# Cross-attention and an eight-expert FFN on one core: x turned earlier, FFN weights prepared over eleven groups, and the expert mask moved from TensorE to VectorE

## The chip, the core and the metric

The kernel runs on one core of a Trainium2 chip. The metric is the device time of one execution in microseconds (us). A core has TensorE (PE in the profile; PEld is its weight loads), VectorE (DVE), ScalarE (ACT), GpSimd (POOL) and the DMA queue of SyncE (SP). They run side by side and meet at semaphores.

## The reference

Input is `x` of 128 batches of 128 tokens by 256, and a context of the same shape. All arithmetic is float32.

```python
x = x + xattn(layernorm(x), ctx, ctx, ...)      # 16 heads of 16
x = x + ffn(layernorm(x), ...)                  # 8 experts, hidden 64

# the FFN, xt being the tokens:
logits = xt @ Wg.T
top1 = argmax(logits)                           # one expert per token
xhat = layernorm without scale
for each expert e:
    h = gelu((xhat * s_e + b_e) @ w1 + bb1)
    y += (top1 == e) * (h @ w2 + bb2)
```

## The kernel before

The batches are worked in 32 groups of four (`GB = 4`, so 512 tokens). A first phase does the attention of all groups and stores `x2` in device memory; a second does the FFN of all groups. Every engine has its own program in a fixed, hand-written order; semaphores join them.

**Attention.** A group has eight steps (`u` from 0 to 7), one per batch and half of the heads. In a step TensorE makes the scores of the unit three ahead (`scores`, L999), the transposed scores (`scoresT`, L1027), and one or two of the ten `item`s of a later group (items 0 and 1 turn the normalised x, 2 and 3 turn the context, 4 to 7 are the query and key projections, 8 and 9 the values), and in even steps the value products `values` (L1041) of the batch before. ScalarE does the exponentials (L593), keeps the turned x (`item(n + 2, 0)`, L557) and normalises the x of the group two ahead (`normalise`, L576, four pieces). VectorE takes the row maxima (`maxima`, L744, L747, L749) that gate the next scores, and the low parts of x and context (`lower`, L770). A float32 operand is kept as two parts, high and low, and multiplied in three products.

VectorE also prepares the FFN weights during attention (`ffn_weights`): per quarter (a *chunk*) a scaling for the first two, a high part and a low part, in steps 4, 5 and 6 of groups 1 to 4; six small ones on the gate weights and `b2` in steps 0 to 6 of group 5.

**FFN.** All eight experts' hidden units (4 pieces `m` of 128 rows, so two experts per piece) are computed for every token, and those of the experts not chosen have to come out as zero. For that, `mask` (L1223) adds to the sum in PSUM one more product per piece, of `far_sel` with `offhotT` (one-hot minus one), which puts −2^30 on every expert that is not chosen; gelu makes it zero. In a group TensorE does `hidden` (24 products of 512 columns, L1216), four of `mask`, `output` (48 products of 256 columns, L1235, and four for the bias, L1238), the turning of the next x (L1182), `gate` (L1191), `turn_logits` (L1197) and `turn_onehot` (L1203). ScalarE does the gelus (L647), keeps the one-hot rows twice (`keep_onehot`, L636, as `offhotT`; `keep_onehot_by_e`, L639, as `onehotT`), keeps the turned x (L632) and copies x2 into the output buffer (L653). VectorE splits each hidden piece into its high part (L853) and low part (L855), normalises the x of the next group (L311, four pieces), takes its statistics (L298, L304), picks the expert (`route`, five small instructions) and adds the output (`add`, L847). GpSimd works out the scale of the normalisation (`ffn_norm`, L504 to L516) and one low part of x (L520). The DMA queue loads x2 (L275) and stores the output (L281).

Of the kernel before, what the change touches and what calls it, by code (L numbers as in the profile page):

```python
# [29 lines left out]
def xattn_moe(nc, x, ctx_in, wq, bq, wk, bk, wv, bv, wo, bo, wg, ln_s, ln_b, w1, b1, w2, b2, out):  # L30
# [13 lines left out]
    assert T == P and D == 256 and GROUPS % 2 == 0 and GROUPS > 4 and GROUPS * GB == BATCH  # L44
# [19 lines left out]
    with ExitStack() as stack:  # L64
# [84 lines left out]
        onehot = sb("onehot", [P, GB, 3, EP], BF16)  # L149
        onehotT = [sb(f"onehotT{n}", [3 * EP, GT], BF16) for n in range(2)]  # L150
        offhotT = [sb(f"offhotT{n}", [3 * EP, GT], BF16) for n in range(2)]
# [92 lines left out]
        f_ld = [sem(f"ffn_x2_loaded{n}") for n in range(2)]  # L244
# [12 lines left out]
        o_ps = [st_ps[:, 0:D], st_ps[:, 512:512 + D]]  # L257
# [11 lines left out]
        def ffn_load(sp, n):  # L269
            src = x2_v[n]  # L270

            wait(sp, f_xn, at(GB, n - 2, GB))
            wait(sp, f_cp, at(1, n - 2, 1))
            sp.wait_ge(st_x2[n % 2], (n // 2 + 1) * 16)
            sp.dma_start(xin[n % 2][:], src).then_inc(f_ld[n % 2], 16)  # L275

        def ffn_sync(sp):
            def store(n):
                dst = out_v[n]
                sp.wait_ge(f_out, at(GB, n, GB))  # L280
                sp.dma_start(dst, xb[n % 2][:]).then_inc(f_st[n % 2], 16)  # L281

            def group(n):
                if n + 3 <= LAST:
                    ffn_load(sp, n + 3)
                store(n)

            ffn_load(sp, 2)
            for n in range(GROUPS):
                group(n)  # L290
            for n in range(2):
                sp.wait_ge(f_st[n], 8 * GROUPS)

        def ffn_stats_of(dve, n):
            v = nc.vector
            dve.wait_ge(f_ld[n % 2], (n // 2 + 1) * 16)
            for b in range(GB):
                v.bn_stats(stats[:, b, :], xin[n % 2][:, b, :]).then_inc(f_bn, 1)  # L298

            for b in range(GB):  # L300
# [5 lines left out]
        def ffn_normalise(dve, n):  # L306
# [3 lines left out]
            for b in range(GB):  # L310
                v.tensor_scalar(xn[:, b, :], xin[n % 2][:, b, :], mv[:, b, 0:1], rstd[:, b:b + 1],  # L311
# [6 lines left out]
        def _(sp):  # L318
# [74 lines left out]
            def group(g):  # L393
# [3 lines left out]
                if 1 <= g <= 4:  # L397
                    load_chunk(g - 1)
# [30 lines left out]
        def _(pool):  # L429
# [70 lines left out]
            def ffn_norm(n):  # L500
# [4 lines left out]
                pool.wait_ge(f_v1, one)  # L505
                g.tensor_tensor(rstd[:], ve[:], neg_half[:], ALU.pow).then_inc(f_r1, 1)
# [9 lines left out]
                g.tensor_tensor(rstd[:], rstd[:], rstd2[:], ALU.mult).then_inc(f_r12, 1)  # L516

# [7 lines left out]
            lo_of_xT(0)  # L525

            def ffn_group(n):
                more = n < LAST
                if n + 2 <= LAST:
                    ffn_norm(n + 2)  # L530
                if more:
                    lo_of_xT(n + 1)
# [6 lines left out]
        def _(act):  # L539
# [31 lines left out]
            def normalise(n):  # L571
                act.wait_ge(s_shift, at(1, n, 1))

                wait(act, s_pp, at(ITEMS, n - 1, 2))
                for b in range(GB):
# [58 lines left out]
            def keep_onehot(n):  # L634
                act.wait_ge(f_ot, at(1, n, 1))
                a.activation(offhotT[n % 2][:], onehotT_ps(n), ACT.Copy, bias=-1.0).then_inc(f_ote, 1)  # L636
# [12 lines left out]
            def copy(n):  # L649

                act.wait_ge(f_ld[n % 2], (n // 2 + 1) * 16)
                wait(act, f_st[n % 2], (n // 2) * 16)
                a.copy(xb[n % 2][:], xin[n % 2][:]).then_inc(f_cp, 1)  # L653

            def group(n):
                more, more2 = n < LAST, n + 2 <= LAST
                for u in range(UNITS):
                    nxt = later(n, u, 2)
                    done = turned_at(n, u)
                    if done and u % 2 == 0:  # L660
                        keep_attn(*done)
                    if u % 2 == 0 and turned_at(n, u + 1):
                        keep_pvT(*turned_at(n, u + 1))
                    if more2 and u == 4:
                        item(n + 2, 0)
# [7 lines left out]
                    if more2 and u == 3:  # L673
                        normalise(n + 2)
# [18 lines left out]
            keep_attn(LAST, GB - 1)  # L693
            def ffn_group(n):
                if n > 0:
                    keep_onehot(n)
                gelu(n, 0)
                gelu(n, 1)
                if n > 0:
                    keep_onehot_by_e(n)  # L700
                if n < LAST:
                    for c in range(C):
                        keep_xT(n + 1, c)
                for m in range(2, MC):
                    gelu(n, m)
                if n < LAST:
                    if n == 0:
                        act.wait_ge(st_x2[1], 8 * GROUPS)
                    copy(n + 1)

            for n in range(GROUPS):
# [4 lines left out]
        def _(dve):  # L716
# [67 lines left out]

            def ffn_weights(n, u):
                last = slice(2 * EP, 3 * EP)
                if n in (1, 2) and u == 4:
                    full = w_chunk[:].rearrange("p (e h) -> p e h", h=HID)
                    dve.wait_ge(s_wf, 16 * n)
                    v.tensor_tensor(full, full, ecols[:, n - 1, E:2 * E].unsqueeze(2).broadcast_to([P, E, HID]),  # L790
                                    ALU.mult).then_inc(s_ffw, 1)
                elif n in (1, 2, 3, 4) and u == 5:
                    dve.wait_ge(s_wf, 16 * n)
                    wait(dve, s_ffw, FFW_FREE[n - 1] + (n < 3))
                    v.tensor_copy(ffn_chunk(n - 1, 0).bitcast(F32R), w_chunk[:]).then_inc(s_ffw, 1)
                elif n in (1, 2, 3, 4) and u == 6:
                    wait(dve, s_ffw, FFW_FREE[n - 1] + (n < 3) + 1)
                    v.tensor_tensor(ffn_chunk(n - 1, 1).bitcast(F32R), w_chunk[:], ffn_chunk(n - 1, 0),
                                    ALU.subtract).then_inc(s_ffw, 1)
                elif n == 5 and u == 0:  # L800
                    v.memset(wg_pad[:].rearrange("p c e -> p (c e)"), 0.0).then_inc(s_ffw, 1)
                elif n == 5 and u == 1:
                    dve.wait_ge(s_ffw, FFW - 6)
                    v.tensor_copy(wg_pad[:, :, 0:E], ecols[:, :, 0:E]).then_inc(s_ffw, 1)
                elif n == 5 and u == 2:
                    dve.wait_ge(s_b2, 16 * 3)
                    v.tensor_copy(b2p[:], b2f[:]).then_inc(s_ffw, 1)
                elif n == 5 and u == 3:
                    dve.wait_ge(s_ffw, FFW - 4)
                    v.tensor_tensor(b2r[:], b2f[:], b2p[:], ALU.subtract).then_inc(s_ffw, 1)  # L810
                elif n == 5 and u in (4, 5):
                    part = slice((u - 3) * EP, (u - 2) * EP)
                    dve.wait_ge(s_ffw, FFW - 3)
                    v.tensor_copy(b2p[part, :], b2r[part, :]).then_inc(s_ffw, 1)
                elif n == 5 and u == 6:
# [26 lines left out]
            def add(n, b):  # L842
# [4 lines left out]
                v.tensor_tensor(xr, xr, o_ps[b % 2], ALU.add).then_inc(f_out, 1)  # L847

            def split_hidden(n, m):

                dve.wait_ge(f_he, at(MC, n, m + 1))
                hi, lo = hT_hi[n % 2][:, m, :], hT_lo[n % 2][:, m, :]
                v.tensor_copy(hi.bitcast(F32R), hidden32[m]).then_inc(f_hh, 1)  # L853
                dve.wait_ge(f_hh, at(MC, n, m + 1))
                v.tensor_tensor(lo.bitcast(F32R), hidden32[m], hi, ALU.subtract).then_inc(f_hl, 1)  # L855
# [105 lines left out]
            residual(LAST, GB - 1)  # L961
            def ffn_group(n):
                more = n < LAST
                if 0 < n < LAST:
                    ffn_normalise(dve, n + 1)
                if 0 < n <= LAST - 2:
                    ffn_stats_of(dve, n + 2)
                for m in range(MC):
                    split_hidden(n, m)
                if n == 0:  # L970
                    ffn_stats_of(dve, 2)
                add(n, 0)
                if more:
                    split_xT(n + 1)
                add(n, 1)
                if more:
# [365 lines left out]
```

## Time and profile before

| | |
|---|---|
| median of 3 runs | 1468.85 us (1468.51 to 1470.84) |
| the profiled execution | 1470.98 us, its span 1468.8 us |
| mean granted TensorE clock | 0.992 |
| PE busy | 1409.6 us, 96% |
| PEld busy | 1206.0 us, 82% |
| DVE busy | 1172.8 us, 80% |
| ACT busy | 866.1 us, 59% |
| POOL busy | 465.4 us, 32% |

The span runs from the first to the last instruction; the execution's own time holds 2.2 us more. A busy share is the mean over two phases with different limits, so each phase is looked at by itself. Starts of instructions count from the span's start. An instruction's row says what ended the idle time before it, behind an arrow.

### The profile page before, as it was taken

How to read it: one execution, taken by the hardware profiler on the slowest of the kernel's cores; microseconds unless marked ns; L12 is line 12 of the kernel's file. 1: busy time of each engine (PE TensorE's matmuls, PEld its weight loads, DVE VectorE, ACT ScalarE, POOL GpSimd, SP SyncE). 2: the span in 40 equal slices, each digit the busy share in tenths (PEclk: the TensorE clock that was granted, in tenths of full speed). 3: DMA queues.
4: the chain of work that ended last, by engine and by line, in shares of the span. 5: the costliest groups of instructions: out<-in, count | busy, mean ns of one | idle time of the engine just before them, and what ended most of it. 6: DMA issues, size and time to landing. Idle time of an engine off the chain costs nothing.

```text
span 1468.8 us, 39587 instructions
## 1 busy us (share of the span) xinstructions
PE 1409.6 (96%) x15438; PEld 1206.0 (82%) x15438; DVE 1172.8 (80%) x2880; ACT 866.1 (59%) x1451; POOL 465.4 (32%) x602
## 2 busy tenths in 40 slices
PE   6799999999999999999999999989999999999998
PEld 5688878888888888888888888867888888888887
DVE  4688888888888888888888888777777777777775
ACT  5466667777777777777777777753343333334342
POOL 4222322223223332323232323223333343433340
PEclk8899999999999999999999999999999999999999
DMA  7566755566556656665666566512222222221211
GB/s 187 119 161 174 178 154 147 158 167 177 154 162 172 179 143 174 171 178 145 169 174 168 146 167 172 156 32 87 72 73 73 73 73 73 72 73 64 81 59 43
DMA packets 150480, 190.89 MB, mean 130 GB/s; under 512 B 17631, under 2 KB 101146, under 8 KB 150298
## 3 DMA queue, kind: packets, MB, share of 16 engines
q1 hardware_dynamic: 150298, 188.38, 47.2%
q8 instruction: 125, 2.05, 0.6%
q14 instruction: 57, 0.47, 0.1%
HBM read 53.01 MB, written 33.55 MB: 59 GB/s over the span
## 4 chain that ended last, share of the span: by engine, by line
PE 73%; DVE 14%; issue 6%; ACT 6%; DMA 1%; POOL 0%; SPq 0%; ACTq 0%; DVEq 0%
PE st_ps L1235 13%; PE s_ps L1216 12%; PE pp_ps L1093 9%; DVE negmax L744 6%; PE s_ps L999 6%; PE pp_ps L1066 6%; PE st_ps L1027 6%; PE pv_ps L1041 5%; PE pp_ps L1101 4%; PE pv_ps L1049 3%; DVE cT_lo L770 3%; ACT xn L576 2%; PE s_ps L1223 2%; PE pp_ps L1182 2%; DVE negmax_wide L747 2%
## 5 line engine op out<-in xcount | busy, mean ns | idle before, releaser
L593 ACT ACTIVATE pT<-st_ps 128x1024 f32<-128x1024 f32 x256 | 263.1, 1028 | 130.3 <-PE st_ps L1027 130.3
L744 DVE TENSOR_REDUCE negmax<-s_ps 128x8 f32<-128x1024 f32 x256 | 311.3, 1216 | 29.1 <-PE s_ps L999 28.9
L1235 PE MATMUL st_ps<-w_hi,q_packed 128*128 128x256 f32 x1024 | 215.8, 296 | 0.2
L472 POOL TENSOR_TENSOR xb<-xin,bo_all 128x256 f32<-128x256 f32 x128 | 91.2, 734 | 273.8 <-DMA x_scratch<-xb 163.1
L1235 PEld LDWEIGHTS st_ps<-w_hi,q_packed 128*128 128x128 f32 x1024 | 167.8, 189 | 10.3 <-issue 6.0
L999 PE MATMUL s_ps<-k_packed,q_packed 96*128 96x128 bf16 x2048 | 157.9, 220 | 18.5 <-issue 8.3
L1216 PE MATMUL s_ps<-k_packed,w_hi 128*128 128x512 f32 x512 | 171.5, 423 | 0.6 <-ACT pT L647 0.6
L460 POOL TENSOR_TENSOR q_parts<-q,q_parts 128x1024 bf16<-128x1024 f32 x32 | 68.5, 2141 | 298.5 <-ACT q_parts L587 298.5
L1027 PE MATMUL st_ps<-q_packed,k_packed 98*128 98x128 bf16 x2048 | 158.4, 220 | 2.5 <-DMA q_packed<-negmaxT 2.4
L999 PEld LDWEIGHTS s_ps<-k_packed,q_packed 96*128 96x128 bf16 x2048 | 127.5, 98 | 39.4 <-DVE negmax L744 20.0
L636 ACT ACTIVATE offhotT<-pv_ps 96x512 bf16<-96x512 bf16 x31 | 18.4, 592 | 222.8 <-PE pv_ps L1203 222.8
L1027 PEld LDWEIGHTS st_ps<-q_packed,k_packed 98*128 98x128 bf16 x2048 | 120.5, 98 | 29.8 <-issue 26.1
L1235 PE MATMUL st_ps<-w_lo,q_packed 128*128 128x256 f32 x512 | 142.4, 278 | 0.0
L1041 PE MATMUL pv_ps<-pT,v 128*32 128x128 f32 x4096 | 138.6, 276 | 0.0
L647 ACT ACTIVATE pT<-s_ps,c 128x512 f32<-128x512 f32 x128 | 84.6, 686 | 67.0 <-PE s_ps L1223 66.1
L551 ACT COPY uvT<-pv_ps 128x512 f32<-128x512 f32 x128 | 75.2, 587 | 76.3 <-PE pv_ps L1041 76.3
L1041 PEld LDWEIGHTS pv_ps<-pT,v 128*32 128x32 f32 x4096 | 104.1, 109 | 13.4 <-issue 0.3
L778 DVE TENSOR_TENSOR xb<-xb,pp_ps 128x256 f32<-128x256 f32 x128 | 53.5, 418 | 65.1 <-PE pp_ps L1066 65.1
L853 DVE CAST q_packed<-pT 128x512 fp32r<-128x512 f32 x128 | 54.5, 425 | 59.1 <-ACT pT L647 59.1
L1216 PEld LDWEIGHTS s_ps<-k_packed,w_hi 128*128 128x128 f32 x512 | 89.9, 191 | 14.1 <-ACT pT L647 1.1
L1235 PEld LDWEIGHTS st_ps<-w_lo,q_packed 128*128 128x128 f32 x512 | 96.6, 189 | 0.8
L847 DVE TENSOR_TENSOR xb<-xb,st_ps 128x256 f32<-128x256 f32 x128 | 53.7, 420 | 50.9 <-PE st_ps L1238 50.7
(181 smaller groups left out, 3489.7 us busy)
## 6 DMA issues: line engine op xcount, KB each, us to landing
q_packed<-q_parts SPq DMA_DIRECT2D x192, 256.0 KB, 3.9
k_packed<-k_parts SPq DMA_DIRECT2D x192, 256.0 KB, 4.6
xin<-in_x_dram SPq DMA_DIRECT2D x32, 512.0 KB, 3.9
cin<-in_ctx_dram SPq DMA_DIRECT2D x32, 512.0 KB, 4.0
x_scratch<-xb SPq DMA_DIRECT2D x32, 512.0 KB, 4.6
xin<-x_scratch SPq DMA_DIRECT2D x32, 512.0 KB, 3.8
out_dram<-xb SPq DMA_DIRECT2D x32, 512.0 KB, 2.9
q_packed<-negmaxT SPq DMA_DIRECT2D x128, 8.0 KB
```

The lines of the kernel that those rows point to most:

```text
L472: last = g.tensor_tensor(xb[n % 2][:, b, :], xin[n % 2][:, b, :], bo_all[:], ALU.add)
L551: a.copy(uvT[:], pv_ps[:]).then_inc(s_uv, 1)
L593: a.activation(pT[u % 2][:], st_ps[:], ACT.Exp, scale=DH ** -0.5).then_inc(s_exp, 1)
L647: a.activation(hidden32[m], h_ps[m % 2], ACT.Gelu, bias=c1[:, m:m + 1]).then_inc(f_he, 1)
L744: v.tensor_reduce(own, s_ps[:].rearrange("p (h s) -> p h s", s=P), AX_X, ALU.max, negate=True).then_inc(s_red, 1)
L999: mm = t.matmul(s_ps[:, j * P:(j + 1) * P], packed[0][n % 2][0:KP, slot(m, j), tok], packed[1][n % 2][0:KP, slot(m, j), tok], start=True, ...
L1027: mm = t.matmul(st_ps[:, j * P:(j + 1) * P], packed[1][n % 2][0:KP + 2, slot(m, j), tok], packed[0][n % 2][0:KP + 2, slot(m, j), tok], sta ...
L1041: mm = t.matmul(pv_ps[strip:strip + HP, block:block + P], v1[n % 2][:, b, h, :], pT[m][:, j * P:(j + 1) * P], start=True, stop=True)
L1066: mm = t.matmul(y_ps, aT[b % 2][i][:, c, :].bitcast(F32R), woT[j][:, c, :].bitcast(F32R), start=(c == 0 and i == j), stop=(c == C - 1 and ...
L1093: mm = t.matmul(ps[:], w[i][:, c, k % 2 * P:(k % 2 + 1) * P].bitcast(F32R), src[j][:, c, :].bitcast(F32R), start=(c == 0 and i == j), stop ...
L1216: t.matmul(h_ps[m % 2], w[:, c, e, :].bitcast(F32R), x[n % 2][:, c, :].bitcast(F32R), start=(k == 0 and c == 0), stop=False)
L1235: t.matmul(o, h[n % 2][:, m, tok].bitcast(F32R), w[:, m, :].bitcast(F32R), start=(m == 0 and k == 0), stop=False)
```

## The change

In attention, at step 4 TensorE turns the first half of the next x (item 0) before the value products, and ScalarE keeps it before it keeps the value products' result; ScalarE's four normalisations move apart, two at the end of step 2 and two in step 3. The FFN weights are prepared over groups 1 to 11, at steps 3 and 6, by the same instructions, and their four loads go out in groups 1, 3, 5 and 7.

In the FFN the four `mask` products go, except in group 0. In their place the one-hot rows, 0 and 1 in bfloat16, are copied by DMA to the 64 rows of each expert: a group has eight copies (`load_mask`), each of one row of `onehotT` to 64 rows of `mask_rows`, which lie in buffers that attention no longer uses. VectorE multiplies each gelu result by them (`mask_hidden`). ScalarE makes the high part of the hidden pieces (`hidden_hi`) and normalises x (`ffn_normalise_by_shift`), and keeps the one-hot rows once. Routing runs one group earlier and the x2 loads have five buffers. The outputs of all four batches are summed side by side in four banks.

```diff
+            def load_mask(n):
+                sp.wait_ge(f_oh, at(1, n, 1))
+                wait(sp, f_hm, at(MC, n - 3, MC))
+                for m in range(MC):
+                    for e in range(EC):
+                        row = EC * m + e
+                        sp.dma_start(mask_rows[n % 2][e * HID:(e + 1) * HID, m, :],
+                                     onehotT[n % 2][row:row + 1, :].unsqueeze(1).broadcast_to([1, HID, GT])
+                                     ).then_inc(f_ml[m // 2], 16)
             def group(n):
-                if n + 3 <= LAST:
-                    ffn_load(sp, n + 3)
+                if n + XF <= LAST:
+                    ffn_load(sp, n + XF)
+                if n < LAST:
+                    load_mask(n + 1)
                 store(n)
...
@@ ScalarE, attention
+                    if more2 and u == 4:
+                        item(n + 2, 0)
                     if u % 2 == 0 and turned_at(n, u + 1):
                         keep_pvT(*turned_at(n, u + 1))
-                    if more2 and u == 4:
-                        item(n + 2, 0)
...
                     if more2 and u == 3:
-                        normalise(n + 2)
+                        normalise(n + 2, range(GB // 2, GB))
...
+                    if more2 and u == 2:
+                        normalise(n + 2, range(GB // 2))
...
@@ ScalarE, FFN
+            def keep_onehot_by_e(n):
+                act.wait_ge(f_ot, at(1, n, 1))
+                for loaded in f_ml:
+                    wait(act, loaded, ML * (n - 2))
                 a.copy(onehotT[n % 2][:], onehotT_ps(n)).then_inc(f_oh, 1)
+            def hidden_hi(n, m):
+                act.wait_ge(f_hm, at(MC, n - 1, m + 1))
+                a.copy(hT_hi[n % 2][:, m, :].bitcast(F32R), hidden32[m]).then_inc(f_hh, 1)
             def ffn_group(n):
-                if n > 0:
-                    keep_onehot(n)
                 gelu(n, 0)
+                hidden_hi(n, 0)
                 gelu(n, 1)
...
+                hidden_hi(n, 1)
+                gelu(n, 2)
+                gelu(n, 3)
+                hidden_hi(n, 2)
                 if n < LAST:
+                    keep_onehot_by_e(n + 1)
+                hidden_hi(n, 3)
                 if n < LAST:
                     copy(n + 1)
+                if n + 3 <= LAST:
+                    ffn_normalise_by_shift(n + 3)
...
@@ VectorE, FFN
+            def mask_hidden(n, m):
+                dve.wait_ge(f_he, at(MC, n, m + 1))
+                dve.wait_ge(f_ml[m // 2], ML * n)
+                v.tensor_tensor(hidden32[m], hidden32[m], mask_rows[n % 2][:, m, :], ALU.mult).then_inc(f_hm, 1)
...
@@ TensorE, FFN
             def ffn_group(n):
+                hidden(n, 0)
                 if more:
                     gate(n + 1)
+                hidden(n, 1)
                 if more:
                     turn_logits(n + 1)
+                if n + 2 <= LAST:
+                    for c in range(C):
+                        turn(n + 2, c)
+                hidden(n, 2)
+                hidden(n, 3)
+                outputs(n, range(GB), 0)
+                if more:
+                    turn_onehot(n + 1)
+                for m in range(1, MC):
+                    outputs(n, range(GB), m)
```

The order of instructions as built shows three places.

TensorE in attention, step 4 of an inner group, before (`scores` of the unit ahead, then from `values` on):

```order
L999 MATMUL s_ps<-k_packed,q_packed 128x128 x8
L1041 MATMUL pv_ps<-pT,v 32x128 x16
L1027 MATMUL st_ps<-q_packed,k_packed 128x128 x8
L1087 MATMUL pp_ps<-ident,xn 128x128 x4
L1066 MATMUL pp_ps<-woT_hi,aT_hi 128x256 x2
```

and after the change:

```order
L1113 MATMUL s_ps<-k_packed,q_packed 128x128 x8
L1201 MATMUL pp_ps<-ident,xn 128x128 x4
L1155 MATMUL pv_ps<-pT,v 32x128 x16
L1141 MATMUL st_ps<-q_packed,k_packed 128x128 x8
L1180 MATMUL pp_ps<-woT_hi,aT_hi 128x256 x2
```

The four transposes of x stand ahead of the value products and the transposed scores.

ScalarE in one inner group of the FFN, before (pT is the gelu's output, k and q the turned x):

```order
L636 ACTIVATE offhotT<-pv_ps 96x512
L647 ACTIVATE pT<-s_ps,c 128x512 x2
L639 COPY onehotT<-pv_ps 96x512
L632 COPY q<-pp_ps 128x512 x2
L647 ACTIVATE pT<-s_ps,c 128x512 x2
L653 COPY xb<-xin 128x1024
```

and after the change (q_packed holds the high and low parts of the hidden pieces):

```order
L690 ACTIVATE pT<-s_ps,c 128x512
L700 CAST q_packed<-pT 128x512
L690 ACTIVATE pT<-s_ps,c 128x512
L672 COPY q<-pp_ps 128x512 x2
L700 CAST q_packed<-pT 128x512
L690 ACTIVATE pT<-s_ps,c 128x512 x2
L700 CAST q_packed<-pT 128x512
L682 COPY onehotT<-pv_ps 96x512
L700 CAST q_packed<-pT 128x512
L696 COPY xb<-v 128x1024
L706 ACTIVATE xn<-xin,shift,rstd 128x256 x4
```

The copy of the next group's one-hot rows (L682) stands behind the third high part (L700) of this group, which needs this group's third masked piece.

The DMA queue in one inner group of the FFN, before:

```order
L275 DMA xin<-x_scratch 128x4x256
L281 DMA out_dram<-xb 128x4x256
```

and after:

```order
L286 DMA xin<-x_scratch 128x4x256
L300 DMA k_parts<-onehotT 64x1x512 x8
L292 DMA out_dram<-xb 128x4x256
```

Eight copies of one row to 64 rows stand between the load and the store of each group (k_parts and q_parts in turn are the mask rows).

## Rows read from the trace of the kernel before

**Rows 1.** Busy time by stretch: attention twice, then FFN; columns as its head says.

```profile
core 0: us, PE busy (x) PEld busy (x) DVE busy (x) ACT busy (x) POOL busy (x), PEclk, DMA share, GB/s
70.00:220.00 150.00, 140.84 (x1809) 123.26 (x1811) 127.77 (x287) 104.00 (x176) 43.40 (x50) 0.99 0.63 163
220.00:950.00 730.00, 713.12 (x9325) 624.10 (x9314) 622.99 (x1396) 528.14 (x897) 216.42 (x246) 1.00 0.62 164
1100.00:1400.00 300.00, 300.00 (x2201) 247.60 (x2200) 227.77 (x665) 114.37 (x185) 118.02 (x164) 1.00 0.22 71
```

**Rows 2.** Timeline of the FFN: one-hot copy and mask products, group by group.

```profile
1200.21 0.59 ACT L636 ACTIVATE offhotT<-pv_ps 96x512 bf16<-96x512 bf16 x1 [7.17 <-PE pv_ps L1203]
...
1201.46 0.60 PE L1223 MATMUL s_ps<-offhotT,far_sel 96*128 96x512 bf16 x2
...
1201.91 1.04 PE L1182 MATMUL pp_ps<-ident,xn 128*128 128x128 f32 x8
...
1215.05 0.59 ACT L636 ACTIVATE offhotT<-pv_ps 96x512 bf16<-96x512 bf16 x1 [7.17 <-PE pv_ps L1203]
```

**Rows 3.** Groups of the FFN, 1000 to 1440 us: busy us, mean ns of one.

```profile
L855 DVE TENSOR_TENSOR q_packed<-pT,q_packed 128x512 fp32r<-128x512 f32 x116 | 80.4, 693 | 4.0
L853 DVE CAST q_packed<-pT 128x512 fp32r<-128x512 f32 x117 | 49.8, 426 | 52.1 <-ACT pT L647 52.1
L311 DVE TENSOR_SCALAR xn<-xin,mv,rstd 128x256 f32<-128x256 f32 x120 | 41.6, 409 | 0.0
L632 ACT COPY q<-pp_ps 128x512 f32<-128x512 f32 x30 | 16.2, 599 | 0.0
```

**Rows 4.** Waits of attention, 220 to 950 us: total, times, longest.

```profile
DVE xT_lo L770 <- ACT xT_hi L557: 14.8, 25, 0.7
PEld s_ps L999 <- DVE negmax L744: 10.5, 42, 0.8
PE pp_ps L1066 <- DVE cT_lo L770: 10.1, 25, 0.6
```

**Rows 5.** Timeline of one inner attention group, steps 3 and 4.

```profile
654.57 1.02 ACT L593 ACTIVATE pT<-st_ps 128x1024 f32<-128x1024 f32 x1 [1.00 <-PE st_ps L1027]
655.49 2.06 ACT L576 ACTIVATE xn<-xin,shift,rstd 128x256 f32<-128x256 f32 x4
658.72 0.59 ACT L557 CAST xT_hi<-pp_ps 128x512 fp32r<-128x512 f32 x1
659.34 0.69 DVE L770 TENSOR_TENSOR xT_lo<-pp_ps,xT_hi 128x512 fp32r<-128x512 f32 x1 [0.59 <-ACT xT_hi L557]
```

**Rows 6.** DMA issues: count, KB each, median us from issue to landing.

```profile
out_dram<-xb SPq DMA_DIRECT2D x32, 512.0 KB, 2.9
q_packed<-negmaxT SPq DMA_DIRECT2D x128, 8.0 KB
```

**Rows 7.** Short windows around a copy into two rows, into 16 rows, and a store.

```profile
603.82:604.05 0.23, 0.23 (x4) 0.17 (x2) 0.23 (x1) 0.23 (x1) 0.23 (x2) 1.00 0.16 36
614.50:614.90 0.40, 0.40 (x6) 0.35 (x3) 0.40 (x1) 0.40 (x2) 0.00 (x0) 1.00 0.98 179
...
1214.20:1216.20 2.00, 2.00 (x13) 1.49 (x11) 2.00 (x7) 0.59 (x1) 0.00 (x0) 1.00 0.70 241
```

**Rows 8.** Timeline, the first FFN group: gelu, and the first hidden piece's high part.

```profile
992.01 1.27 ACT L647 ACTIVATE pT<-s_ps,c 128x512 f32<-128x512 f32 x2
...
993.66 0.42 DVE L853 CAST q_packed<-pT 128x512 fp32r<-128x512 f32 x1
```

**Rows 9.** Timeline, the end of the span: last addition and last store.

```profile
1464.91 0.42 DVE L847 TENSOR_TENSOR xb<-xb,st_ps 128x256 f32<-128x256 f32 x1 [1.07 <-PE st_ps L1238]
1465.36 0.37 SPq L281 DMA_DIRECT2D out_dram<-xb  x1
```

**Rows 10.** Timeline of attention group 5: a stretched instruction beside a GpSimd one.

```profile
211.41 2.13 POOL L460 TENSOR_TENSOR k_parts<-k,k_parts 128x1024 bf16<-128x1024 f32 x1
211.42 2.15 DVE L749 TENSOR_TENSOR negmax_wide<-negmax,negmax_wide 128x8 bf16<-128x8 f32 x1
```

More of the change, by code:

```diff
@@ L149, in xattn_moe @@
         onehot = sb("onehot", [P, GB, 3, EP], BF16)
+        v_rows = v1[0][:].rearrange("p b h d -> p (b h d)").rearrange("p (k b d) -> p k b d", k=2, b=GB)
+        xf = [xin[0][:], xin[1][:], cin[:], v_rows[:, 0, :, :], v_rows[:, 1, :, :]]
+        XF = len(xf)
+        mask_rows = [part[:, 0:MC // C, :, :].rearrange("p a c t -> p (a c) t") for part in parts]
         onehotT = [sb(f"onehotT{n}", [3 * EP, GT], BF16) for n in range(2)]
-        offhotT = [sb(f"offhotT{n}", [3 * EP, GT], BF16) for n in range(2)]
+        offhotT = sb("offhotT", [3 * EP, GT], BF16)
         def psum(name, shape, dt=F32):
@@ L569, in item, with normalise @@
                 last.then_inc(s_pe, 1)
[L571 to L575, printed above, removed]
+            def normalise(n, batches=range(GB)):
+                if batches[0] == 0:
+                    act.wait_ge(s_shift, at(1, n, 1))
+                    wait(act, s_pp, at(ITEMS, n - 1, 2))
+                for b in batches:
                     a.activation(xn[:, b, :], xin[n % 2][:, b, :], ACT.Identity, bias=shift[:, b:b + 1],
@@ L785, in ffn_weights, with chunk_lo @@
+            def chunk_lo(k):
+                dve.wait_ge(s_ffw, FFW_FREE[k] + (k < C) + 1)
+                v.tensor_tensor(ffn_chunk(k, 1).bitcast(F32R), w_chunk[:], ffn_chunk(k, 0),
+                                ALU.subtract).then_inc(s_ffw, 1)
             def ffn_weights(n, u):
                 last = slice(2 * EP, 3 * EP)
[L787 to L800, printed above, removed]
@@ L1221, in mask, with output @@
+            def mask(m):
                 if m == 0:
[L1222 to L1223 removed]
+                    pe.wait_ge(f_ote, 1)
+                t.matmul(h_ps[m % 2], far_sel[:, EC * m:EC * (m + 1), :], offhotT[:],
                          start=False, stop=True).then_inc(f_h, 1)
[L1226 to L1227 removed]
+            def output(n, b, m):
+                o = o_ps(n, b)
@@ L1228, in output @@
                 tok = slice(b * T, (b + 1) * T)
-                if parts[0] == 0:
-                    wait(pe, f_out, at(GB, n, b - 1))
-                for m in parts:
-                    if b == 0:
-                        pe.wait_ge(f_hl, at(MC, n, m + 1))
-                    for k, (h, w) in enumerate(((hT_hi, w2_hi), (hT_hi, w2_lo), (hT_lo, w2_hi))):
-                        t.matmul(o, h[n % 2][:, m, tok].bitcast(F32R), w[:, m, :].bitcast(F32R),
-                                 start=(m == 0 and k == 0), stop=False)
@@ L1237, in output @@
-                if parts[-1] == MC - 1:
+                if m == 0:
+                    if n == 0:
+                        wait(pe, f_out, b - 1)
+                    else:
+                        pe.wait_ge(f_out, at(GB, n - 1, b + 1 if n > 1 or b > 1 else b + 3))
+                    if n > 0 and b >= 2 and n + 2 <= LAST:
+                        pe.wait_ge(f_tre, at(C, n + 2, b - 1))
+                if b == 0:
+                    pe.wait_ge(f_hl, at(MC, n, m + 1))
+                for k, (h, w) in enumerate(((hT_hi, w2_hi), (hT_hi, w2_lo), (hT_lo, w2_hi))):
+                    t.matmul(o, h[n % 2][:, m, tok].bitcast(F32R), w[:, m, :].bitcast(F32R),
+                             start=(m == 0 and k == 0), stop=False)
```

255 lines of the change are left out of this document (169 added, 86 removed).

## The prediction

> **What bounds the kernel now.** I read the windows by phase first, since the page's shares mix two phases. In [rows 1] the reader sees that in the FFN (1100 to 1400 us) PE is busy 300.00 of 300 us, DVE 227.8, ACT 114.4, POOL 118.0, and the DMA engines 0.22 of their time at 71 GB/s. The timeline [rows 2] gives the period of an FFN group: the one-hot copy L636 starts at 1200.21 and at 1215.05, so 14.84 us. TensorE alone sets it. In attention PE is busy 713.12 of 730 us between 220 and 950 us, and 140.84 of 150 us before that, so 16.9 and 9.2 us of idle time are all there is to win without taking work away. The waits [rows 4] say who makes the first: TensorE waits for the row maxima (10.5 us for its weight loads) and for the low part of the context (10.1 us), both VectorE's.
>
> **Attention, part by part.** VectorE waits 14.8 us in 25 groups, 0.6 each, for the turned x that ScalarE keeps [rows 4]. [rows 5] show one: L557 starts at 658.72, VectorE's L770 behind it at 659.34 after 0.59 idle. What makes it late is the four normalisations from 655.49 on (2.06 us) and the place behind the value products. Half of them move into the 1.00 us that ScalarE idles before its exponential at 654.57, and the transposes move ahead of the products. VectorE gets up to 0.6 us per group, the two waits of TensorE shrink, and I take half of the 16.9 us: 8. The weight preparation is the same VectorE work, spread thinner; of the 9.2 us of idle time before 220 us, 5.7 are above the later rate (150 x 16.9/730 = 3.5), and I take 2. Part of those 5.7 is one collision, where a 0.17 us VectorE instruction takes 2.15 us beside GpSimd's 2.13 us one [rows 10]; other places of such instructions can lose or meet it. Sum −10, bounds 0 (another wait takes over) and −26 (all idle time).
>
> **FFN, what leaves TensorE.** Two mask products start at 1201.46 and the next thing at 1201.91 [rows 2]: 0.225 us each, 0.9 for four. If nothing else bound, a group would take 14.84 − 0.9 = 13.9 us. VectorE loses four high parts (4 x 0.426) and four normalisations (4 x 0.409) and gains four multiplications of the kind of L855 (4 x 0.693) [rows 3]: −0.6 on 11.3 us a group (227.8 of 300). ScalarE gains four casts of 512 columns (about 0.6, as L632) and four normalisations (a quarter of 2.06 each), less one copy: +3.9 on 5.7 us. Both fit 13.9. GpSimd gains two small instructions.
>
> **FFN, what comes in: eight copies.** Each reads one row of `onehotT` (512 values of bfloat16, 1 KB) and writes 64 rows, 64 KB. The trace has no copy out of one row, so I bound it. From below: the store moves 241 GB/s with the DMA engines busy 0.70, so 344 GB/s at full share, 21.5 per engine [rows 7]; 65.5 KB in 0.2 us, which the 0.4 us of an issue [rows 9] hides. From above by copies that meet in few rows. The copy of the row maxima into two rows moves 36 GB/s [rows 7]. The packing copy into 16 rows, alone at 614.50, moves 179 GB/s at a share of 0.98, so 11.4 GB/s per engine, half of the store's 21.5. I read this as two engines that meet at one place in the memory, which then gives 22.8 GB/s together. In the new copies all engines read one row, so they all meet. I take their nearest rows, not the store: 22.8 to 36, and within that 26.6, since the copy from 128 rows also has 16 engines at work but its engines pass on to other rows. That is 65.5/26.6 = 2.46 us a copy, 19.7 us for eight, with 14.6 and 23.0 as bounds.
>
> The Trainium skill speaks to this. "SBUF — State Buffer", section "Door 1: the DMA port swizzle", has the partitions share 16 ports by fours, and measures 27.6 GB/s for a transfer that touches partitions 0 to 3 alone; rows 0 to 3 would be one port and 4 to 7 another. Its figure would make an estimated 2.37 us a copy and 19.0 for eight, and the end 1698 us. Its section "The DMA setup-cost knee" has a formula by bytes alone, 2 us + bytes/436 GB/s, by which the copies would hide, and the end be that of the first rival.
>
> **What waits for them.** `load_mask(n + 1)` goes out when ScalarE has kept the one-hot rows of group n + 1. That copy stands behind `hidden_hi(n, 2)`, which waits for the third masked piece of group n, which waits for the second half of group n's copies. So there is a loop: copies, mask, high part, keep, copies. Behind the waiting `mask_hidden` on VectorE are all later low parts, the split of the next x and the additions; TensorE's `output` waits for those. The fixed part of a DMA is 2.9 us from issue to landing of a store [rows 6] less 524 KB at 344 GB/s, 1.5, so 1.4. Mask 0.69, high part 0.60, keep 0.58, and 0.3 for the handovers (an estimate, a few at 0.05 to 0.1). The loop takes 1.4 + 19.7 + 2.2 = 23.3 us against 14.84. The x2 load and the store, 1.5 us each, go through the same engines in the 3.6 us of the loop without mask data. TensorE will idle some 9 us of each group; its granted clock was 0.94 in the stretch that holds the collision, where one wait was 1.7 us, so it will fall here too, but it is not in the loop.
>
> **The sum**, against the profiled execution. VectorE's first high part starts at 993.66 [rows 8]. Then about 2.0 us of statistics that now stand ahead, four splits of 1.12 (4.5), 0.3 for logits, 0.8 for the last of the outputs of two batches, 0.4 for the turning and 0.6 for keeping: `load_mask(1)` at 1002.3, less the 10 of attention 992.3. There are 31 loads: 30 loops (699), the last load (1.4 + 19.7 = 21.1), and the end: two masks 1.4, high and low part 1.3, the last quarter of the outputs 1.6, an addition 0.4, and 3.4 from the store's issue at 1465.36 to the span's end [rows 9], together 8.1. The span is 992.3 + 699 + 21.1 + 8.1 = 1720.5; +2.2 around it, and −2.1 for the profiled 1470.98 against the median 1468.85: 1720.6 us. With 14.6 us of copies the loop is 18.2 and the end 1562; with 23.0 it is 26.6 and the end 1823.
>
> **Rivals.** *The copies are hidden.* If rows can be read by all engines at a good rate, they go out at 0.4 us each [rows 9] and land within 5 us, and the first half is due some 6.5 us after the one-hot rows are kept (three quarters of the outputs and the first hidden piece lie between). Then TensorE sets the period: 13.9 us, −0.9 x 31 = −28, and −10 from attention: 1431 us. It decides at the point where the loop equals 14.84: eight copies in 11.2 us, 1.4 each, 47 GB/s out of one row. For it speaks that the store's engines run at full speed side by side; against it the halved engines of the packing copy and the 36 GB/s into two rows. Chance 0.20. *Handovers eat the gain.* The copies hide, but the split of a hidden piece now goes VectorE, ScalarE, VectorE, and the last low part comes close. TensorE has the fourth hidden piece 7.3 us into a group (24 products at 0.23 are 5.6, gate and turns 1.7) and wants the last low part 4.5 us later, at 11.8. That part is ready at 10.9: gelu and mask 1.6, the two high parts and the one-hot copy that ScalarE does in turn 1.3 more, low part 0.7. Slack 0.9 us. Two casts late put up to 1 us back in each group: 1431 + 31 = 1462, and the middle 1447. Chance 0.07, of which 0.02 within 0.2% of no change. *The loop binds* as above, chance 0.73.
>
> **How the numbers follow.** The likeliest case gives 1720.6, its own range being 1560 to 1823. To leave no more than 2 in 10 out, the range has to reach to the other cases: 1430 to 1800. What differs by less than 0.2% (3 us) can't be told from no change here. Faster 0.25, same 0.02, slower 0.73.
>
> **What would show it.** Right: one period of about 23 us in the FFN, VectorE's masks waiting for the DMA that writes the mask rows, TensorE busy some 60%, DMA share high for most of a group at a low GB/s (about 27 for the copies alone), issue to landing growing from copy to copy. Wrong: a period of 13.9 to 14.8 us with no wait for these copies. In attention: VectorE's wait for the turned x gone, TensorE's waits at L999 and L1066 (in the old numbering) smaller, and the idle time before 220 us spread. The number falls with the rate out of one row: each 1 GB/s around 26.6 is worth about 23 us.

## The result, and the profile after

The changed kernel takes 1676.06 us (median of 4 runs, 1674.09 to 1676.81) against 1468.97 for the kernel before on the same chip: ratio 1.1405, 95% interval 1.1388 to 1.1423. It is 207 us slower.

The page of its profiled execution (span 1672.2 us): busy time, 40 slices, the chain that ended last.

```profile
PE 1457.9 (87%) x15314; PEld 1252.7 (75%) x15314; DVE 1166.5 (70%) x2760; ACT 992.6 (59%) x1664; POOL 446.3 (27%) x662
...
PE   6999999999999999999999887777777777777776
...
PEclk9999999999999999999999998888888888889888
DMA  6576656656565666757565447777777777777765
GB/s 179 134 186 152 179 148 175 176 156 171 150 179 153 175 169 160 185 149 178 147 179 153 129 73 75 74 75 75 75 75 75 73 66 67 72 75 75 63 49 57
...
PE 44%; DMA 18%; SPq 18%; DVE 13%; issue 4%; ACT 3%; DVEq 0%; ACTq 0%
```

The reader is to see two lines against each other: in the FFN (the right half) the DMA engines are busy seven tenths of the time, and yet move 75 GB/s; in attention they move twice that at six tenths. And 36% of the chain that ended last now runs through transfers (DMA) and through the issues of SP's queue (SPq).

Windows of attention and FFN, which answer to [rows 1] (columns as there):

```profile
70.00:220.00 150.00, 146.90 (x1919) 127.95 (x1916) 131.62 (x295) 110.16 (x187) 45.12 (x53) 1.00 0.65 166
220.00:950.00 730.00, 715.58 (x9307) 624.55 (x9305) 626.71 (x1410) 533.54 (x895) 216.62 (x246) 1.00 0.63 164
...
1100.00:1400.00 300.00, 225.28 (x1445) 189.42 (x1445) 152.30 (x403) 131.24 (x222) 70.63 (x140) 0.87 0.77 71
```

TensorE's idle time fell from 9.2 to 3.1 us in the first and from 16.9 to 14.4 in the second. In the FFN no engine is full. The waits from 1000 to 1600 us say for what they stand still:

```profile
ACT q_packed L700 <- DVE pT L940: 208.1, 56, 6.4
...
PE t_ps L1314 <- DVE logitT L928: 131.5, 28, 5.1
DVE pT L940 <- DMA q_parts<-onehotT: 124.3, 28, 5.7
DVE pT L940 <- DMA k_parts<-onehotT: 121.0, 27, 5.5
```

L940 is `mask_hidden`; it waits 245 us for the copied rows (`q_parts` and `k_parts` are the two buffers of `mask_rows`), ScalarE waits for it in `hidden_hi`, and TensorE for the logits, whose copy stands behind the mask in VectorE's order. One loop, in the chain that ended last (start, length, what):

```profile
1249.68 0.70 DVE pT L940
1250.39 0.02 issue
1250.41 0.04 ACT q_packed L700
1250.45 0.48 issue
1250.94 0.58 ACT onehotT L682
1251.52 0.02 issue
1251.54 0.47 SPq L300
...
1253.33 1.62 SPq L300
1254.95 0.04 issue
1254.99 2.36 SPq L300
1257.35 0.04 issue
1257.39 2.36 SPq L300
1259.75 0.04 issue
1259.80 1.90 SPq L300
1261.69 0.04 issue
1261.73 9.44 DMA k_parts<-onehotT
...
1271.27 0.70 DVE pT L940
```

From mask to mask it is 21.6 us, and the starts of L682 give a mean period of 21.67 (14.84 before, [rows 2]). From the first issue (1251.54) to the last landing (1271.17) it is 19.6 us, all the rest 2.0. The fifth and sixth issue take 2.36 us each, and 65.5 KB in 2.36 us are 27.8 GB/s: in this loop the queue takes a new copy only as fast as an old one leaves. Short windows in the middle of the copies show the rate:

```profile
1256.00:1258.00 2.00, 2.00 (x23) 1.30 (x22) 1.47 (x8) 0.69 (x1) 0.37 (x2) 1.00 0.79 26
1258.00:1260.00 2.00, 0.99 (x5) 0.46 (x3) 0.00 (x0) 0.00 (x0) 1.69 (x5) 1.00 0.84 28
```

26 to 28 GB/s with the DMA engines 0.8 busy.

### The profile page after: what moved, and what is told of

Same layout as the page of the kernel before. It is cut to its first block, busy times and chain, and to the rows that moved or that the text cites. A ratio compares the mean times of both kernels' runs of the same rounds, so it can differ in the third digit from the quotient of the medians.

```text
span 1672.2 us, 40098 instructions
## 1 busy us (share of the span) xinstructions
PE 1457.9 (87%) x15314; PEld 1252.7 (75%) x15314; DVE 1166.5 (70%) x2760; ACT 992.6 (59%) x1664; POOL 446.3 (27%) x662
## 4 chain that ended last, share of the span: by engine, by line
PE 44%; DMA 18%; SPq 18%; DVE 13%; issue 4%; ACT 3%; DVEq 0%; ACTq 0%
SPq L300 18%; DMA k_parts<-onehotT 9%; DMA q_parts<-onehotT 9%; PE pp_ps L1207 8%; PE pp_ps L1180 6%; PE pv_ps L1155 6%; PE s_ps L1113 6%; PE st_ps L1141 5%; PE pp_ps L1215 5%; DVE negmax L818 5%; PE pv_ps L1163 3%; DVE cT_lo L844 2%; DVE negmax_wide L821 1%; DVE pT L940 1%; PE pp_ps L1201 1%
## 5 line engine op out<-in xcount | busy, mean ns | idle before, releaser
L818 DVE TENSOR_REDUCE negmax<-s_ps 128x8 f32<-128x1024 f32 x256 | 311.4, 1216 | 23.3 <-PE s_ps L1113 23.1
L700 ACT CAST q_packed<-pT 128x512 fp32r<-128x512 f32 x124 | 76.9, 620 | 234.0 <-DVE pT L940 234.0
L1333 PE MATMUL s_ps<-k_packed,w_hi 128*128 128x512 f32 x512 | 192.7, 473 | 5.1 <-ACT pT L690 5.1
L940 DVE TENSOR_TENSOR pT<-pT,k_parts 128x512 f32<-128x512 f32 x64 | 42.8, 689 | 145.9 <-DMA k_parts<-onehotT 139.3
L1358 PE MATMUL st_ps<-w_hi,q_packed 128*128 128x256 f32 x528 | 124.3, 297 | 22.8 <-DVE q_packed L948 21.5
L1314 PE MATMUL t_ps<-ident,logitT 128*128 128x128 f32 x31 | 13.9, 448 | 141.0 <-DVE logitT L928 141.0
L940 DVE TENSOR_TENSOR pT<-pT,q_parts 128x512 f32<-128x512 f32 x60 | 40.1, 689 | 135.1 <-DMA q_parts<-onehotT 135.1
L1333 PEld LDWEIGHTS s_ps<-k_packed,w_hi 128*128 128x128 f32 x512 | 109.1, 230 | 31.2 <-issue 6.2
L1314 PEld LDWEIGHTS t_ps<-ident,logitT 128*128 128x128 f32 x31 | 5.4, 174 | 154.0 <-DVE logitT L928 154.0
L948 DVE TENSOR_TENSOR q_packed<-pT,q_packed 128x512 fp32r<-128x512 f32 x128 | 88.6, 693 | 43.5 <-ACT q_packed L700 40.7
L1358 PEld LDWEIGHTS st_ps<-w_hi,q_packed 128*128 128x128 f32 x528 | 92.9, 190 | 30.4 <-DVE q_packed L948 27.5
```

Source lines behind the costliest of these rows:

```text
L818: v.tensor_reduce(own, s_ps[:].rearrange("p (h s) -> p h s", s=P), AX_X, ALU.max, negate=True).then_inc(s_red, 1)
L940: v.tensor_tensor(hidden32[m], hidden32[m], mask_rows[n % 2][:, m, :], ALU.mult).then_inc(f_hm, 1)
L1333: mm = t.matmul(h_ps[m % 2], w[:, c, e, :].bitcast(F32R), x[n % 2][:, c, :].bitcast(F32R), start=(k == 0 and c == 0), stop=(n > 0 and k == ...
L1358: t.matmul(o, h[n % 2][:, m, tok].bitcast(F32R), w[:, m, :].bitcast(F32R), start=(m == 0 and k == 0), stop=False)
```

## The experiments

Eleven kernels. "Before" is measured anew beside each set.

**1 and 2. The attention half, and its weights alone.** The first is the kernel before with all attention edits and the FFN of before. The second has only the other places of the weight preparation:

```diff
-                if 1 <= g <= 4:
-                    load_chunk(g - 1)
+                if g in (1, 3, 5, 7):
+                    load_chunk(g // 2)
```

and `ffn_weights` at steps 3 and 6 of groups 1 to 11.

> The attention half of the change alone (x turned ahead of the value products, the normalisations moved apart, FFN weights over eleven groups) with the FFN of before. The first gelu of the FFN started 11.3 us earlier after the change than before (980.7 against 992.0 us). If that is all the attention half's, the time is 1468.9 - 11 = 1458 us (1455 to 1460). Rival: 2 to 3 us of the 11.3 come from the new order of the first FFN group, then 1460 to 1462. A second rival: nothing is won, as another wait takes over, 1469.

> Only the preparation of the FFN weights is spread over groups 1 to 11; the turned x stays where it was. TensorE's idle time between 70 and 220 us fell from 9.2 to 3.1 us with both, and that between 220 and 950 us by 2.5 us only. If the weights give the first and the turned x the second, this one is worth 6 us: 1463 us (1461 to 1465). Rival: the early idle time goes by the turned x as well, then 1467 to 1469 here.

Measured: both 1462.5 us, ratio 0.9959 (0.9947 to 0.9972); the weights alone 1463.8, ratio 0.9972 (0.9959 to 0.9984). So the half is worth 6 us, not 11: with one and the same attention program the first FFN instruction of ScalarE, `first_gelu`, starts at 977.7, 979.5 or 982.4 us in three profiles of this study, so one profile can't carry a difference of 2 or 3 us.

**3 and 4. Which place the rows are read from.** Four copies in place of eight, each out of two rows, 33 or 65 partitions apart. Rows 32 to 39 and 64 to 71 hold the same one-hot values as rows 0 to 7.

```diff
                 for m in range(MC):
-                    for e in range(EC):
-                        row = EC * m + e
-                        sp.dma_start(mask_rows[n % 2][e * HID:(e + 1) * HID, m, :],
-                                     onehotT[n % 2][row:row + 1, :].unsqueeze(1).broadcast_to([1, HID, GT])
-                                     ).then_inc(f_ml[m // 2], 16)
+                    row = EC * m
+                    sp.dma_start(mask_rows[n % 2][:, m, :],
+                                 onehotT[n % 2][row:row + 65 + 1:65, :].unsqueeze(1).broadcast_to([EC, HID, GT])
+                                 ).then_inc(f_ml[m // 2], 16)
```

> The changed kernel with four copies of 128 KB a group in place of eight of 64 KB; each writes the two halves of a piece from two rows that lie 33 partitions apart and hold the same values as before. Same bytes, half as many DMAs. Theory (the rate out of one place of the memory, 29 GB/s, binds, and these two rows are one place): the loop stays, 1676 us (1650 to 1690). Rival A (a fixed price for each DMA of about 2.4 us): copies 9.8 us, loop under TensorE's 13.9 us, so 1676 - 31 x (21.67 - 13.9) = 1435 us. Rival B (two rows are two places, each with its own rate): the same 1435 us. The Trainium skill, page on SBUF, section on the DMA port swizzle, says that partitions 32 apart share a port, which speaks for 1676.

> As the kernel with rows 33 apart, but the second row of each copy lies 65 partitions from the first. Same DMAs, same bytes, same packets, only the source row differs. Theory (place binds, and these rows are two places): twice the rate, copies 9 to 10 us, loop 13.0 to 14.5 us, so 1425 to 1455 us. Rival A (fixed price for each DMA): 1435 as well, but then the other kernel is as fast. Rival C (each 1 KB packet costs 490 ns whatever the row, or all rows are one place): 1676 us in both. The Trainium skill, page on SBUF, section on the DMA port swizzle, puts partitions 64 apart on different ports, which speaks for the first.

Measured: 33 apart 1788.2 us, ratio 1.2178 (1.2161 to 1.2195), period 25.2; 65 apart 1487.5, ratio 1.013 (1.011 to 1.0151), period 15.6. Same instructions, 300 us apart by the row alone. Both times lie outside what was expected (1650 to 1690, and 1425 to 1455): the rates are 24 and 47 GB/s where 29 and twice that were taken. Windows inside the copies, first 33 apart, then 65:

```profile
1201.00:1207.00 6.00, 5.93 (x42) 4.34 (x40) 3.28 (x12) 1.05 (x2) 1.92 (x4) 0.87 0.11 24
```

```profile
1200.00:1205.00 5.00, 5.00 (x41) 3.52 (x39) 3.41 (x14) 1.69 (x4) 2.48 (x4) 1.00 0.14 47
```

24 against 47 GB/s. Neither expectation foresaw the share of 0.11 to 0.14: that is two of the 16 engines (2/16 = 0.125). So two engines on one place give 24 GB/s together (the prediction read 22.8 off the packing copy), on two places 23.5 each. The changed kernel's copies keep most of the engines busy and give 26 to 28 out of one row: more engines hardly help. That the price is one for each DMA (rival A) falls with the slower of the two, and that each packet has its price whatever the row (rival C) with the faster. The Trainium skill, "SBUF — State Buffer", "Door 1: the DMA port swizzle", has partitions 32 apart on one port and 64 apart on two; these two runs agree. The page "DMA: Bandwidth & Descriptors" of the Trainium skill says in "Why a DMA increments its semaphore by 16 and not by 1" that the number of engines is the largest up to 16 that divides the slowest dimension of both patterns; here these are two rows read and 128 rows written, so two engines, and the shares agree.

**5. Out of device memory.** Only the source is another:

```diff
+                sp.dma_start(onehot_dram[n % 2], onehotT[n % 2][0:E, :]).then_inc(f_md, 16)
+                sp.wait_ge(f_md, 16 * n)
                 for m in range(MC):
                     for e in range(EC):
                         row = EC * m + e
                         sp.dma_start(mask_rows[n % 2][e * HID:(e + 1) * HID, m, :],
-                                     onehotT[n % 2][row:row + 1, :].unsqueeze(1).broadcast_to([1, HID, GT])
+                                     onehot_dram[n % 2, row:row + 1, :].unsqueeze(1).broadcast_to([1, HID, GT])
                                      ).then_inc(f_ml[m // 2], 16)
```

> The changed kernel, but the one-hot rows are first stored in device memory (8 KB, one DMA, waited for), and the same eight copies of 64 KB read them there in place of one row of on-chip memory. Destinations, bytes, packets and number of copies stay. Theory (the rate out of one place of on-chip memory binds): a copy costs only its issue, 0.6 us; loop: keep 0.6, store 2.5, eight issues 4.7, landing 2.5, mask and high part 1.5, together 11.8 us, under TensorE's 13.9; then 1468 - 7 (attention) - 28 (masks) = 1433 us (1425 to 1450). Rival A (the destination, rows of 1 KB, or the number of packets binds): 1676 us plus the store's 2.5 in each of 30 loops, 1750. Rival B (device memory too gives one row slowly to 16 engines): between the two.

Measured: 1434.3 us, ratio 0.9766 (0.9751 to 0.9782): 35 us faster than before. Its FFN window, and its DMA issues with the time to landing:

```profile
1100.00:1400.00 300.00, 298.98 (x2273) 259.03 (x2272) 237.97 (x621) 202.88 (x347) 133.60 (x210) 1.00 0.37 111
```

```profile
k_parts<-onehot_scratch SPq DMA_DIRECT2D x128, 64.0 KB, 2.6
q_parts<-onehot_scratch SPq DMA_DIRECT2D x120, 64.0 KB, 2.6
```

In the changed kernel the same copies take this long:

```profile
k_parts<-onehotT SPq DMA_DIRECT2D x128, 64.0 KB, 9.2
```

All eight issues take 4.92 us together instead of 12.40. TensorE is busy 298.98 of 300 us again, in a period of 13.81 us. Destination, packets, count of copies and VectorE's masks are those of the changed kernel, so none of them is what made it slow.

**6. Opening the loop.** The next one-hot rows are kept ahead of the third high part:

```diff
-                hidden_hi(n, 2)
                 if n < LAST:
                     keep_onehot_by_e(n + 1)
+                hidden_hi(n, 2)
```

with one pair of semaphores for each of the two mask buffers, since copies of two groups are now under way.

> The changed kernel with ScalarE's copy of the next one-hot rows ahead of the third high part in place of behind it (and the semaphores of the copies one set for each of the two buffers). So the next copies no longer wait for the second half of these. Theory (a loop of latency and rate): with the loop opened, the rate alone sets the period: eight copies at 2.3 us, 18.0 to 18.5, and about 1.5 for the load and the store between them: 20.0 us a group in place of 21.67, and 1676 - 31 x 1.7 = 1624 us (1600 to 1645). Rival A (the rate alone sets 21.67 already, load and store included): 1676, no change. Rival B (the wait on TensorE's side sets it): no change either.

Measured: 1606.1 us, ratio 1.0943 (1.0916 to 1.0969), periods of 18.4 to 20.9, mean 19.3. So 2.4 us of the 21.67 were the loop's latency; the rest is the rate, and even without the loop it is above 14.84.

**7. TensorE's wait.**

```diff
-                mask_hidden(n, 0)
                 if more:
                     keep_logits(n + 1)
+                mask_hidden(n, 0)
```

> The changed kernel with VectorE's copy of the logits ahead of the first masked piece in place of behind it. TensorE waits 4.7 us in each group for it while VectorE waits for the DMA. Theory (TensorE isn't in the loop): that wait goes or moves behind the hidden pieces, the period stays 21.67 and the time 1676 us (1673 to 1679). Rival B (TensorE's wait, and the lower clock that it brings, are in the loop): up to 4.7 us less a group, 1530 us.

Measured: 1677.1 us, ratio 1.1421 (1.1402 to 1.1440), period 21.68. The wait for the logits has gone from the list and two others have come (1100 to 1400 us), with TensorE as idle as it was (busy 225.95 of 300 us, and 225.28 in the changed kernel):

```profile
PE s_ps L1333 <- ACT pT L690: 38.0, 14, 3.4
PE st_ps L1358 <- DVE q_packed L948: 36.1, 14, 4.2
```

The longest wait of the engine that used to be the bound told nothing of the cause.

**8 and 9. Fewer copies out of device memory.** Four copies of 128 KB each (two pieces in one), once with the one-hot rows kept early as in 6, once late as in the change:

```diff
...
+                for k in range(2):
+                    for e in range(EC):
+                        src = onehot_dram[n % 2, EC * 2 * k + e:EC * 2 * k + e + EC + 1:EC, :]
+                        sp.dma_start(mask_rows[n % 2][e * HID:(e + 1) * HID, 2 * k:2 * k + 2, :],
+                                     src.unsqueeze(0).broadcast_to([HID, 2, GT])).then_inc(f_ml[k], 16)
```

> As the kernel that goes by way of device memory, but with four copies of 128 KB a group in place of eight of 64 KB, and the copy of the next one-hot rows ahead of the third high part. If the kernel by way of device memory is bound by TensorE already, this is the same as that, 1433 us (1425 to 1450); if its loop still binds, this takes 2.4 us of issues and 1.3 us of wait out of it and is up to 31 x 3.7 = 115 us faster than that one, down to 1433.

> By way of device memory with four copies of 128 KB a group, and the copy of the next one-hot rows where the changed kernel has it, behind the third high part. The kernel with the same four copies and that copy ahead had a period of 14.52 us against 13.81 with eight copies and that copy behind. If the place of the copy of the one-hot rows costs the 0.7 us (ScalarE waits for the turned rows while the third high part is due), this one is at 13.81 again: 1434 us (1431 to 1437). Rival (fewer, larger copies land later): 1453 us.

Measured: early 1453.0 us, ratio 0.9897 (0.988 to 0.9915), period 14.52, a miss; late 1431.1, ratio 0.9759 (0.9744 to 0.9774), period 13.82. The move that won 70 us while the copies were the bound costs some 20 us once TensorE is (0.70 us in each of 31 groups). In the early one (1100 to 1400 us) ScalarE stands before the turned one-hot rows while the third high part is due, and the output products wait for the low part made from it, 0.65 us a group:

```profile
ACT onehotT L685 <- PE pv_ps L1323: 18.9, 20, 0.9
...
PEld st_ps L1361 <- DVE q_packed L951: 13.0, 20, 0.7
```

Of eight or four copies nothing can be told (0.9766 and 0.9759, the intervals overlap).

**10. The turned x alone.** The edits to `normalise`, `even` and ScalarE's group, weights as before.

> The kernel before with only the turned x ahead of the value products and the normalisations moved apart; weights prepared as before. Both parts together measured 5.5 us faster than before, the weights alone 4.2. If the parts add up, this one is worth 1 to 2 us: 1466.5 to 1467 us, hardly to be told from no change. Rival (the prediction's split, 8 us for this part and 2 for the weights): 1460 us.

Measured: 1463.6 us, ratio 0.9981 (0.9973 to 0.9990), so 2.8 us. With the weights' 4.1 it makes 6.9 for the 6.0 of both. In the windows TensorE's idle time from 70 to 220 us is 9.2 us in the kernel before, 5.6 with the turned x alone, 5.1 with the weights alone and 3.1 with both; from 220 to 950 us it is 16.9, 13.9, 17.5 and 14.0. So the early idle time goes by either part, and the later one by the turned x only, within what one profile can carry.

**11. Half the bytes.**

```diff
-                        sp.dma_start(mask_rows[n % 2][e * HID:(e + 1) * HID, m, :],
-                                     onehotT[n % 2][row:row + 1, :].unsqueeze(1).broadcast_to([1, HID, GT])
+                        sp.dma_start(mask_rows[n % 2][e * HID:(e + 1) * HID, m, 0:GT // 2],
+                                     onehotT[n % 2][row:row + 1, 0:GT // 2].unsqueeze(1).broadcast_to([1, HID, GT // 2])
                                      ).then_inc(f_ml[m // 2], 16)
```

> The changed kernel with each of the eight copies half as wide: 256 of the 512 columns, so 512 bytes out of the one row into each of 64 rows. Left out: the mask of the other half of the tokens, which is multiplied by what lies in the buffer. As many copies and packets as before, half the bytes. Theory (bytes out of one place, 29 GB/s): copies 9 to 10 us, loop 13.0 to 13.5, so TensorE binds at 13.8: 1434 us (1430 to 1460). Rival (each packet costs its 490 ns when 16 engines meet, whatever its size): 1676 us.

Measured: 1433.5 us, ratio 0.9781 (0.9767 to 0.9794), period 13.82. Windows inside the copies of one group:

```profile
1209.00:1212.00 3.00, 3.00 (x23) 2.65 (x22) 2.56 (x7) 1.51 (x4) 1.67 (x1) 1.00 0.66 26
1212.00:1214.00 2.00, 2.00 (x23) 1.28 (x22) 1.66 (x9) 0.69 (x1) 0.55 (x2) 1.00 0.67 53
```

26 GB/s as with packets of twice the size: it is bytes that the place gives out at a rate. The second window holds the change from rows 0 to 3 to rows 4 to 7; it is taken up below.

## Why the prediction was right, step by step

**The bound and its cause: right.** The loop of copies, mask, high part and keep sets the period, and inside it the rate out of one row. Experiments 5 and 11 take the rate away and the loop vanishes; 3 and 4 change only the row; 6 opens the loop and 2.4 us go. The signs named are there: one period, masks waiting for the DMA, the DMA engines 0.77 busy at 71 GB/s, the time from issue to landing growing over the first four copies (4.5, 6.3, 8.1 and 9.3 us in the loop from 1251.54 on) and then 9.1 to 9.4. TensorE is 75% busy, not 60: its clock is lower (0.87 mean), so the same work takes longer, and the period is shorter.

**The size of the loop: 23.3 predicted, 21.67 measured.** The rest of the loop was right (2.2, measured 2.0). The term that was mis-sized is the 21.1 us for the copies, measured 19.6: 524 KB in 19.6 less the 1.4 taken as fixed is 28.8 GB/s, where 26.6 was taken within 22.8 and 36. In the sum thirty loops were 49 us too long, the last load 1.5 and the start 0.9. Two things take part of that back: the end was 3.0 us too short, and the profiled execution lies 2.0 us under the median, where the sum had it 2.1 over. That leaves the miss of 44.5.

The landings of one loop show where the higher mean comes from. The eight copies land at 1256.06, 1258.40, 1260.84, 1262.61, 1264.20, 1266.60, 1268.93 and 1271.17. The first is 4.5 us behind its issue, where 1.4 + 2.46 = 3.9 was reckoned. Five of the seven steps are 2.2 to 2.4 us (2.46 predicted), and the two before and behind the fourth landing are 1.77 and 1.59, together 1.6 us less than predicted. That is the place where the copies pass from rows 0 to 3 to rows 4 to 7. Over all 31 groups of copies the medians of the seven steps are 2.38, 2.43, 1.79, 1.58, 2.41, 2.35 and 2.30. The rate goes up for 1 us there:

```profile
1261.50:1262.50 1.00, 0.00 (x0) 0.00 (x0) 0.00 (x0) 0.00 (x0) 0.03 (x1) 0.50 0.82 79
1262.50:1263.50 1.00, 0.00 (x0) 0.00 (x0) 0.80 (x2) 0.07 (x1) 0.00 (x0) 0.50 0.79 27
```

Experiment 11 shows the same in its second window, 53 GB/s. That some engines read the old rows and some the new at that moment is the likely reason; why it is 79 and not twice 27 stays open. The sum had no such moment in it. That the rate itself came out so close (26 to 28 in the windows) is partly luck: no row gave a value between the bounds of 22.8 and 36, and 26.6 was a choice between them.

**The start and the end.** The first copies go out at 991.4 us (992.3 predicted). Behind the last landing come 11.1 us (1661.1 to 1672.2), 8.1 predicted: the two last pieces wait for the same copies, so half the output products and not a quarter stand behind them. TensorE had waited 2.93 us for them, and most of them ran at half the clock (0.51, so 1.2 of 2.4 GHz, in the window; then the first and the last product):

```profile
1664.20:1667.60 3.40, 3.40 (x19) 3.12 (x18) 0.84 (x2) 0.00 (x0) 0.00 (x0) 0.51 0.01 2
```

```profile
1663.25 0.39 PE L1358 MATMUL st_ps<-w_hi,q_packed 128*128 128x256 f32 x1 [2.93 <-DVE q_packed L948]
...
1668.08 0.28 PE L1361 MATMUL pp_ps<-b2p,onehotT 96*128 96x256 bf16 x1
```

**Attention: −10 predicted, −6 measured** (interval −7.8 to −4.1), inside its bounds, but the split was wrong: 8 for the turned x and 2 for the weights, measured 2.8 and 4.1. The step that failed took TensorE's two waits to shrink with VectorE's wait for the turned x [rows 4]. That wait is gone, and the two of TensorE stayed, as the waits of the changed kernel from 220 to 950 us show:

```profile
PE pp_ps L1180 <- DVE cT_lo L844: 10.6, 25, 0.7
PEld s_ps L1113 <- DVE negmax L818: 10.0, 44, 0.9
...
DVE xT_lo L844 <- ACT xT_hi L596: 0.2, 1, 0.2
```

VectorE's 14.6 us were slack of its own. Most of what went was idle time of TensorE before 220 us, by both parts (experiment 10).

**What leaves TensorE: right.** −0.9 a group, a period of 13.9; experiment 5 has 13.81, so −1.0. The rival with hidden copies was priced at 1431 and both kernels with a fast source come out at 1431.1 and 1434.3 (by their ratios 1433.5 and 1434.5 against the prediction's 1468.85). *Handovers eat the gain* does not happen in them; experiment 8 shows how near it was, with one copy of 0.58 us moved. The point from which it decides, 47 GB/s, was somewhat low: the kernel that reads just 47 GB/s has a period of 15.6, not 14.84. Its copies take 13.7 us from the first issue to the last landing (1197.58 to 1211.27), where 524 KB at 47 are 11.2, so 2.5 and not 1.4 us are fixed there, partly issues.

**The two rules that were weighed.** The 2.37 us a copy by the port's figure of 27.6 GB/s (Trainium skill, "SBUF — State Buffer", "Door 1: the DMA port swizzle") were the nearer estimate: an issue in the queue's steady state takes 2.36 us, and 1698 is nearer than 1720.6. The formula by bytes alone (same page of the Trainium skill, "The DMA setup-cost knee") gives an estimated 2.15 us to landing for 64 KB; device memory as the source shows 2.6, one row of on-chip memory 4.5 for the first copy of a loop and 9.1 to 9.4 from the fourth on, behind its neighbours in the queue.

## What to carry to other kernels

A broadcast out of one row of on-chip memory is priced by bytes written over the rate of the one place read (here 24 to 28 GB/s), not by the number of engines. Going by way of device memory turned 14% slower into 2.4% faster. Two distant source rows, with two engines, doubled the rate but left the kernel 1.3% slower than before; all engines on several distant rows was not tried. A moved instruction has to be priced against what binds: the same move won 70 us in one kernel and lost some 20 in the next. Where DMA engines are busy at a low GB/s, look at their source rows before anything else.

## What was not expected of the hardware

- Two engines reading one place give 24 GB/s, most of the 16 reading one row 26 to 28; two engines on two places 47.
- A copy whose source has 2 as its outermost dimension keeps two of 16 engines busy (share 0.14).
- With slow copies in the queue, unrelated issues slow down as well. These rows of SP's queue in the changed kernel are eight copies, then a store and a load of 512 KB; by device memory (experiment 5) the store's issue takes 1.06 and the load's 0.43 us.

```profile
1251.54 12.40 SPq L300 DMA_DIRECT2D k_parts<-onehotT  x8
1263.98 2.35 SPq L292 DMA_DIRECT2D out_dram<-xb  x1
1266.45 2.37 SPq L286 DMA_DIRECT2D v<-x_scratch  x1
```

- The granted clock fell with TensorE's waits: 0.50 (1.2 of 2.4 GHz) from 1261.5 to 1267.5 us, behind an idle time that began at 1259.0. It cost nothing in the loop, since TensorE was not part of it. At the end of the span TensorE was on the path, and the products at 0.51 above cost some 1.7 us more than at full clock (an estimate, half of the 3.4 us).

```profile
1261.50:1267.50 6.00, 3.85 (x14) 3.47 (x15) 3.61 (x10) 2.90 (x5) 0.03 (x1) 0.50 0.81 36
```
